# Attention with a gated recurrence on one core: the maxima of the scores are rounded and turned by a rounded product

## The chip, the cores and the metric

One core of a Trainium2 chip runs the whole program in one launch. The metric is device time in microseconds; lower is better. Of several runs the median is given.

## The reference

The input is x of 8 batches with 512 rows of 128. It is normalised by rows (layer norm). Of the result xn two things are computed and added to x: an attention of 16 heads of 64, and a gated recurrence over the 8 batches.

```python
def attn(data, W_qkv, b_qkv, W_out, b_out):      # data: (8, 512, 128)
    qkv = data @ W_qkv + b_qkv                   # 3 * 1024 columns
    q, k, v = (a.reshape(n, l, 16, 64) for a in split(qkv))
    scores = jnp.einsum('nqhd,nkhd->nhqk', q, k)
    attention = jax.nn.softmax(scores / jnp.sqrt(64.), axis=3)
    out = jnp.einsum('nhql,nlhd->nqhd', attention, v).reshape(n, l, 1024)
    return out @ W_out + b_out

def ffn(x, ...):                                 # one step for each batch
    def step(c, xt):
        ft = sigmoid(xt @ wf.T + c @ uf.T + bf)
        it = sigmoid(xt @ wi.T + c @ ui.T + bi)
        gt = tanh(xt @ wc.T + c @ uc.T + bc)
        return ft * c + it * gt, None
    c_final, _ = lax.scan(step, c0, x)
    return tanh(einsum('tbi,oi->tbo', x, wo) + c_final @ uo.T + bo)

result = x + attn(xn, ...) + ffn(xn, ...)
```

## The kernel before

The 16 heads of a batch are 8 pairs; a pair's two heads lie on partitions 0 to 63 and 64 to 127. A batch is 4 stretches (`j` from 0 to 3), each with two pairs, `s` = 2j and 2j + 1; `t` = 8n + s counts the pairs over all batches. The batches run in a loop of the device for n from 1 to 6, with batch 0 and batch 7 written out apart (`batches`). Each engine has its own stream, in an order written out by hand; semaphores join them.

Operands of the scores and projections are split into a rounded part (`QH`, `KH`, `XH`, `WH`, of type float32r) and a rounded rest (`QL`, `KL`, ...), and three rounded products make one. Products of values, of the sums and of the turns take operands of full precision (float32).

For a stretch two pairs ahead, TensorE makes the raw scores of each block of 128 queries once with the rounded parts alone (`score_maxima`, into `mx`), and VectorE takes the largest of each row, negated, into two columns of `NM` (`maxima`, line 592). `NM` is 128x64: two heads, two pairs, four blocks make 16 columns, the others are zero. When a stretch's 16 columns are there, TensorE turns them with one product: `NM` is the stationary operand, the identity the moving one, and 64x128 come out in `mx` (`turn_max`, line 851; for the very first pair `turn_first`, line 926). VectorE copies 16 rows of that into `TM` (`take_max`, line 599, and line 661), two DMAs of SyncE's queue lay them into `MROW`, and the last product of each block's scores adds them to every row (line 871), ahead of the exponential on ScalarE.

At the end of each stretch TensorE runs the values: for each of two pairs, four blocks of keys times two heads (`values`, line 879), the even pair into the bank `pv`, the odd one into `misc`. A product's stationary operand has 64 columns; head 0 goes to partitions 0 to 63 of the bank and head 1 to 64 to 127. The turn for the next stretch stands in the middle of the first pair: `values(n, t, s, (0, 1))`, `turn_max(t + 2)`, `values(n, t, s, (2, 3))`. In the middle of the second pair stand the four sums of the divisors (`four_sums`, line 898) with 32 columns each. There are 33 turns: the first at the start, the second ahead of the first batch's stretch 0, and one in each stretch but the last of batch 7.

What waits near the turn:
- In batches 1 to 7 the values of `misc` wait, in stretch 0, for the tanh of the recurrence, and in stretch 2 for the batch's output rows (`finish`, line 638, VectorE).
- In batch 0 they wait for the state of the recurrence: VectorE runs `take_max`, then `update` (line 573), ScalarE copies and rounds the state (lines 385 and 380), VectorE makes the low half (line 557).
- VectorE's order in stretch 2 is: low halves of two pairs (lines 578, 585), `take_max`, the divisors (line 624), `finish`.

ScalarE begins with seven issues of DMAs, a square root that brings in the table (line 354), and the deviation of batch 0 (`deviation`, line 359). GpSimd makes the identity first (lines 254 to 256), then ones, pads and the zeros of `NM` (line 263).

Of the kernel before, what the change touches and what calls it, by code (L numbers as in the profile page):

```python
# [5 lines left out]
def build_block(nc, data, W_qkv, b_qkv, W_out, b_out, wf, uf, bf, wi, ui, bi, wc, uc, bc, wo, uo, bo, in_c, out):  # L6

    f32 = mybir.dt.float32
    f32r = mybir.dt.float32r
# [4 lines left out]
    P = 128  # L14
# [3 lines left out]
    HD = P // 2  # L18
# [17 lines left out]
    with ctx:  # L36
        def sb(name, shape, dt=f32):
            return ctx.enter_context(nc.sbuf_tensor(name, shape, dt))

        def sem(name):  # L40
            return ctx.enter_context(nc.semaphore(name))

        ident = sb("ident", [P, P])
# [31 lines left out]
        gwL = sb("gwL", [P, 8, P], f32r)  # L75
        DH = sb("DH", [P, L], f32r)
        DL = sb("DL", [P, L], f32r)
        NM = sb("NM", [P, HD])
        TM = sb("TM", [4 * TB, P])
        epst = sb("epst", [P, 1])  # L80
        spare = sb("spare", [P, 2])
# [15 lines left out]
        mx = ctx.enter_context(nc.psum_tensor("mx", [P, 2, L], f32))  # L97
# [21 lines left out]
        ld_b, ld_w, ld_wo = sem("ld_b"), sem("ld_w"), sem("ld_wo")  # L119
        ld_x = [sem("ld_x12"), sem("ld_x34"), sem("ld_x57")]  # L120
        ld_W = [sem("ld_Wq"), sem("ld_Wk"), sem("ld_Wv")]
        id0, id1, ones_set, pads_set, pads_nm, eps_set = sem("id0"), sem("id1"), sem("ones_set"), sem("pads_set"), sem("pads_nm"), sem("eps_set")
        bias_tr, bias_col, bias_half, bias_fold, bias_fin = (sem("bias_tr"), sem("bias_col"), sem("bias_half"),
                                                             sem("bias_fold"), sem("bias_fin"))
        gw_tr, gw_raw, gw_hi, gw_lo = sem("gw_tr"), sem("gw_raw"), sem("gw_hi"), sem("gw_lo")
        first_turned, first_tm, d_first = sem("first_turned"), sem("first_tm"), sem("d_first")
# [16 lines left out]
        q_lo, k_lo, red_done, max_turned, tm_done, den_used, r16_done, rd_done, out_done = (  # L143
            sem("q_lo"), sem("k_lo"), sem("red_done"), sem("max_turned"), sem("tm_done"), sem("den_used"), sem("r16_done"),
            sem("rd_done"), sem("out_done"))
# [107 lines left out]
        def _(pool):  # L253
# [6 lines left out]
            nc.gpsimd.memset(MROW[:, :, :].bitcast(f32), 0.0).then_inc(pads_set, 1)  # L260
            nc.gpsimd.memset(ONEROW[:, :].bitcast(f32), 0.0).then_inc(pads_set, 1)
            pool.wait_ge(pads_set, 2)
            nc.gpsimd.memset(NM[:, :], 0.0).then_inc(pads_nm, 1)
            for h in range(2):
                nc.gpsimd.memset(ONEROW[AUX[h], :].bitcast(f32), 1.0).then_inc(pads_set, 1)
                pool.wait_ge(pads_set, 3 + h)
# [81 lines left out]
        def _(act):  # L348

            act.dma_start(brow[0:3 * PAIRS, :], b_qkv.rearrange("(c r) -> c r", r=P)).then_inc(ld_b, 16)  # L350
            for i, v in enumerate((b_out, bf, bi, bc, bo, in_c)):
                act.dma_start(brow[B_OUT + i:B_OUT + i + 1, :], v.rearrange("(a r) -> a r", a=1)).then_inc(ld_b, 16)
            act.wait_ge(eps_set, 1)
            nc.scalar.activation(spare[:, 0:1], epst[:, :], ACT.Sqrt)

# [165 lines left out]
        def _(dve):  # L521
# [66 lines left out]
            def maxima(t, s, b, turned=0):  # L588

                wait(dve, max_turned, turned)  # L590
                dve.wait_ge(mx_done, 4 * t + b + 1)
                nc.vector.tensor_reduce(NM[:, 0:4 * TB].rearrange("p (h a b) -> p h a b", h=2, a=2)[:, :, s % 2, b],  # L592
                                        mx[:, :, :], AX.X, ALU.max, negate=True).then_inc(red_done, 1)
# [162 lines left out]
        def _(pe):  # L756
# [91 lines left out]
            def turn_max(t):  # L848

                pe.wait_ge(red_done, 4 * t + 8)  # L850
                nc.tensor.matmul(mx[0:HD, 0, 0:P], NM[:, :], ident[:, :], start=True, stop=True).then_inc(max_turned, 1)

            def scores(n, t, s, u, parts=range(4)):

# [68 lines left out]
            def turn_first():  # L923

                pe.wait_ge(red_done, 4)
                nc.tensor.matmul(mx[0:HD, 0, 0:P], NM[:, :], ident[:, :], start=True, stop=True).then_inc(first_turned, 1)

            turn_x(0)
            pe.wait_ge(ld_b, 16 * 7)
# [22 lines left out]
            for c in range(PAIRS):  # L952
                last = nc.tensor.matmul(pv[:, 0:1], WO[:, c, :], bcol[:, B_V + c:B_V + c + 1],
                                        start=(c == 0), stop=(c == PAIRS - 1))
            last.then_inc(bias_fold, 1)
            pe.wait_ge(pads_nm, 1)
            turn_first()
            pe.wait_ge(ones_set, 1)
            pe.wait_ge(pads_set, 4)
# [12 lines left out]
            def step(n, first, last):  # L972
                for j in range(STRETCHES):
# [4 lines left out]
                    if first and j == 0:  # L978
# [23 lines left out]
                        project(0, 3, 0, q_done, first_q[3])  # L1002
                        project(0, 3, DIM, k_done, first_k[3])
                        turn_max(0)
                        pe.wait_ge(q_lo, 3)
                        pe.wait_ge(k_lo, 3)
# [131 lines left out]
                    if coming:  # L1138
                        if first:
                            pe.wait_ge(xl_done, min(s + 3, N))  # L1140
                        turn_max(t + 2)
# [63 lines left out]
```

## Time and profile before

| | |
|---|---|
| median of 3 runs | 889.63 us (889.49 to 891.8) |
| the profiled execution | 892.3 us, its span 890.5 us |
| granted TensorE clock, mean | 0.994 |
| busy: TensorE products | 846.6 us (95%), 5431 records |
| busy: VectorE, ScalarE, GpSimd | 529.0, 450.4, 568.3 us |
| reductions into NM (line 592) | 256, 1226 ns each |
| products of values (line 879) | 1024 records of about 600 ns, 250.9 us busy |

Times of a row count from the span's start. A record of a product is as long as its operands travel through the array; several are under way at once, so what a product costs is the distance from one start to the next, and not its length. A product of full operands has two records, a rounded one has one. The view of the order of time joins neighbours of one kind: "x8" is eight records, and its duration reaches from the first start to the last end. "[0.69 <-PE mx L851]" is idle time of the engine and what ended it.

### The profile page before, as it was taken

To read this page: it belongs to the slowest core of one execution; us is meant where nothing else is said; L and a number is where in the kernel's file an instruction comes from. 1 tells how busy PE (TensorE), PEld (TensorE's weight loads), DVE (VectorE), ACT (ScalarE), POOL (GpSimd) and SP (SyncE) were. 2 spreads that over 40 slices of the span, in tenths; PEclk is the share of its full clock that TensorE was granted. 3 is DMA by queue.
4 is the path that set the end of the run, shared out by engine and by line. 5 is a ranking of instruction groups with operands and counts; after the bars stand their busy time and mean duration, and the time that the engine had idled before them with its cause. 6 is when DMAs were issued, how large, how long until landed. Compare 5 with 4: busy or idle time off the path is not lost.

```text
span 890.5 us, 15128 instructions
## 1 busy us (share of the span) xinstructions
PE 846.6 (95%) x5431; PEld 497.6 (56%) x5431; DVE 529.0 (59%) x687; ACT 450.4 (51%) x585; POOL 568.3 (64%) x299
## 2 busy tenths in 40 slices
PE   6989999999999999999999999999999999999997
PEld 4555566555656545655656645665556645665442
DVE  6676765566466646666466646666466646666422
ACT  5456465455545524555555525555455525555430
POOL 4637684376567647776567647776567647776465
PEclk9899999999999999999999999999999999999999
DMA  8000000000000000000000000000000000000000
GB/s 236 1 1 1 25 1 1 1 14 26 2 14 14 1 25 12 1 13 24 1 13 13 1 24 13 1 13 24 1 13 13 1 24 13 1 14 1 2 25 12
DMA packets 28491, 14.22 MB, mean 16 GB/s; under 512 B 11154, under 2 KB 26032, under 8 KB 28464
## 3 DMA queue, kind: packets, MB, share of 16 engines
q1 hardware_dynamic: 28416, 13.84, 5.4%
q8 instruction: 17, 0.28, 0.1%
q14 instruction: 10, 0.08, 0.0%
q10 hardware_dynamic: 48, 0.02, 0.0%
HBM read 6.83 MB, written 2.10 MB: 10 GB/s over the span
## 4 chain that ended last, share of the span: by engine, by line
PE 86%; DVE 8%; issue 2%; ACT 2%; POOL 2%; DMA 0%; DVEq 0%; POOLq 0%; ACTq 0%
PE st L863 19%; PE misc L879 13%; PE pv L879 9%; PE st L796 9%; PE mx L844 8%; PE st L871 6%; PE mx L905 6%; PE st L898 3%; DVE NM L592 3%; PE pv L796 2%; PE misc L779 2%; PE misc L796 2%; PE pv L779 1%; DVE KL L578 1%; PE mx L779 1%
## 5 line engine op out<-in xcount | busy, mean ns | idle before, releaser
L592 DVE TENSOR_REDUCE NM<-mx 128x2 f32<-128x1024 f32 x256 | 313.9, 1226 | 183.2 <-PE mx L844 183.1
L426 ACT ACTIVATE probs<-st 128x1024 f32<-128x1024 f32 x256 | 256.8, 1027 | 71.5 <-PE st L871 64.9
L309 POOL TENSOR_TENSOR PSUMK<-probs 128x1024 f32<-128x1024 f32 x64 | 153.4, 2397 | 217.8 <-ACT probs L426 217.8
L315 POOL TENSOR_TENSOR PSUMK<-PSUMK,probs 128x1024 f32<-128x1024 f32 x64 | 152.8, 2387 | 6.1
L322 POOL TENSOR_TENSOR PSUMK<-PSUMK,probs 128x1024 f32<-128x1024 f32 x64 | 152.6, 2385 | 6.1
L879 PE MATMUL misc<-probs,VALL 128*64 128x512 f32 x512 | 125.7, 600 | 12.5 <-DVE RES L638 9.5
L879 PE MATMUL pv<-probs,VALL 128*64 128x512 f32 x512 | 125.2, 608 | 0.2 <-DVE RES L563 0.2
L844 PE MATMUL mx<-KH,QH 64*128 64x512 f32 x512 | 108.0, 415 | 6.7 <-DVE NM L592 6.0
L863 PE MATMUL st<-QH,KH 64*128 64x512 f32 x512 | 105.3, 405 | 0.6 <-ACT probs L426 0.6
L863 PE MATMUL st<-QL,KH 64*128 64x512 f32 x512 | 102.0, 393 | 0.0
L863 PE MATMUL st<-QH,KL 64*128 64x512 f32 x512 | 102.0, 392 | 0.0
L871 PE MATMUL st<-MROW,ONEROW 64*128 64x512 f32 x512 | 101.6, 390 | 0.0
L879 PEld LDWEIGHTS misc<-probs,VALL 128*64 128x64 f32 x512 | 44.0, 136 | 85.9 <-issue 51.2
L844 PEld LDWEIGHTS mx<-KH,QH 64*128 64x128 f32 x512 | 48.3, 184 | 62.6 <-issue 28.8
L298 POOL TENSOR_TENSOR AT<-AT,RD 128x512 f32<-128x512 f32 x49 | 61.5, 1274 | 23.8 <-DVE RD L610 12.4
L418 ACT COPY AT<-pv 128x512 f32<-128x512 f32 x25 | 14.7, 588 | 121.8 <-PE pv L879 121.8
L418 ACT COPY AT<-misc 128x512 f32<-128x512 f32 x24 | 14.1, 586 | 108.8 <-PE misc L879 108.8
L863 PEld LDWEIGHTS st<-QH,KH 64*128 64x128 f32 x512 | 48.3, 185 | 36.5 <-ACT probs L426 29.8
L879 PEld LDWEIGHTS pv<-probs,VALL 128*64 128x64 f32 x512 | 44.5, 137 | 42.6 <-issue 31.4
L616 DVE STREAM_TRANSPOSE SD<-st 128x512 f32<-128x512 f32 x28 | 20.1, 717 | 80.8 <-PE st L898 80.8
L905 PE MATMUL mx<-AT,WO 128*128 128x512 f32 x128 | 57.2, 599 | 9.3 <-DVE NM L592 9.3
L871 PEld LDWEIGHTS st<-MROW,ONEROW 64*128 64x128 f32 x512 | 48.7, 184 | 10.6 <-issue 0.4
(183 smaller groups left out, 1221.0 us busy)
## 6 DMA issues: line engine op xcount, KB each, us to landing
XSH<-XH SPq DMA_DIRECT2D x8, 256.0 KB, 2.4
XSL<-XL SPq DMA_DIRECT2D x8, 256.0 KB, 2.4
RES<-in_L_attn_data_dram SPq DMA_DIRECT2D x8, 256.0 KB, 2.8
out_dram<-RES SPq DMA_DIRECT2D x8, 256.0 KB, 2.3
RX<-R SPq DMA_DIRECT2D x112, 2.0 KB, 1.7
probs<-in_L_attn_W_qkv_dram SPq DMA_DIRECT2D x3, 512.0 KB, 5.6
AT<-in_L_attn_data_dram SPq DMA_DIRECT2D x2, 512.0 KB, 7.1
MROW<-TM SPq DMA_DIRECT2D x62, 4.0 KB
```

The costliest lines, as they stand in the source:

```text
L298: nc.gpsimd.tensor_tensor(AT[:, s % PAIRS, :], unnormalised(first, s), RD[:, s % 2, :], ALU.mult).then_inc(norm_done, 1)
L309: nc.gpsimd.tensor_tensor(PSUMK[:, s % 2, :, :], e[:, :, 0, :], e[:, :, 1, :], ALU.add).then_inc(sum_part, 1)
L315: nc.gpsimd.tensor_tensor(PSUMK[:, s % 2, :, :], PSUMK[:, s % 2, :, :], probs[:, s % 2, :, 2, :], ALU.add).then_inc(sum_part, 1)
L322: nc.gpsimd.tensor_tensor(PSUMK[:, s % 2, :, :], PSUMK[:, s % 2, :, :], probs[:, s % 2, :, 3, :], ALU.add).then_inc(sum_done, 1)
L426: nc.scalar.activation(probs[:, s % 2, :, u, :], st[:, u % 2, :, :], ACT.Exp, scale=SCALE).then_inc(exp_done, 1)
L592: nc.vector.tensor_reduce(NM[:, 0:4 * TB].rearrange("p (h a b) -> p h a b", h=2, a=2)[:, :, s % 2, b], mx[:, :, :], AX.X, ALU.max, negate= ...
L796: last = nc.tensor.matmul(dst, stationary[OWN[h], :], moving[OWN[h], :], start=(slot == 0), stop=(slot == 5))
L844: last = nc.tensor.matmul(mx[:, h, :], QH[OWN[h], s % 4, b * P:(b + 1) * P], KH[OWN[h], s % 4, :], start=True, stop=True)
L863: nc.tensor.matmul(st[:, u % 2, h, :], k[OWN[h], s % 4, b], q[OWN[h], s % 4, :], start=(i == 0), stop=False)
L871: last = nc.tensor.matmul(st[:, u % 2, h, :], ONEROW[OWN[h], :], MROW[OWN[h], s % 2, :], start=False, stop=True)
L879: last = nc.tensor.matmul(value_banks[s % 2][OWN[h], :], VALL[:, kb, s * P + h * HD:s * P + (h + 1) * HD], probs[:, s % 2, h, kb, :], star ...
L905: last = nc.tensor.matmul(dst, WO[:, c, :], AT[:, c, :], start=(c == 0), stop=(c == PAIRS - 1))
```

## The change

`NM` becomes float32r, so that VectorE rounds the maxima where it writes them. A second identity, `identr`, of type float32r, is filled once by a copy on ScalarE ahead of the first square root. The turns take `NM` and `identr`; their place in TensorE's stream is the same, and TensorE waits once for `identr` ahead of the first turn.

```diff
-        NM = sb("NM", [P, HD])
+        NM = sb("NM", [P, HD], f32r)
+        identr = sb("identr", [P, P], f32r)
...
-            nc.gpsimd.memset(NM[:, :], 0.0).then_inc(pads_nm, 1)
+            nc.gpsimd.memset(NM[:, :].bitcast(f32), 0.0).then_inc(pads_nm, 1)
...
                 act.dma_start(brow[B_OUT + i:B_OUT + i + 1, :], v.rearrange("(a r) -> a r", a=1)).then_inc(ld_b, 16)
+            act.wait_ge(id1, 1)
+            nc.scalar.copy(identr[:, :], ident[:, :]).then_inc(idr, 1)
             act.wait_ge(eps_set, 1)
...
             def turn_max(t):
 
                 pe.wait_ge(red_done, 4 * t + 8)
-                nc.tensor.matmul(mx[0:HD, 0, 0:P], NM[:, :], ident[:, :], start=True, stop=True).then_inc(max_turned, 1)
+                nc.tensor.matmul(mx[0:HD, 0, 0:P], NM[:, :], identr[:, :], start=True, stop=True).then_inc(max_turned, 1)
...
             def turn_first():
 
                 pe.wait_ge(red_done, 4)
-                nc.tensor.matmul(mx[0:HD, 0, 0:P], NM[:, :], ident[:, :], start=True, stop=True).then_inc(first_turned, 1)
+                nc.tensor.matmul(mx[0:HD, 0, 0:P], NM[:, :], identr[:, :], start=True, stop=True).then_inc(first_turned, 1)
...
             pe.wait_ge(pads_nm, 1)
+            pe.wait_ge(idr, 1)
             turn_first()
```

## Rows read from the trace of the kernel before

**Rows 1.** The page: the chain that ended last, shares by engine.
```profile
PE 86%; DVE 8%; issue 2%; ACT 2%; POOL 2%; DMA 0%; DVEq 0%; POOLq 0%; ACTq 0%
```
**Rows 2.** Line 851: who waited for it (us in total, times).
```profile
  DVE TM L599: 16.2, 12
```
**Rows 3.** Order of time, TensorE, values with a turn: start, us, engine, line.
```profile
322.28 1.94 PE L879 MATMUL pv<-probs,VALL 128*64 128x512 f32 x8
324.04 0.27 PE L851 MATMUL mx<-ident,NM 128*64 128x128 f32 x1
324.05 0.64 PE L879 MATMUL pv<-probs,VALL 128*64 128x512 f32 x1
324.15 0.27 PE L851 MATMUL mx<-ident,NM 128*64 128x128 f32 x1
324.26 1.88 PE L879 MATMUL pv<-probs,VALL 128*64 128x512 f32 x7
325.82 0.75 PE L879 MATMUL misc<-probs,VALL 128*64 128x512 f32 x2
```
**Rows 4.** Order of time, TensorE, last stretch of batch 7: values without a turn.
```profile
873.29 1.02 PE L905 MATMUL mx<-AT,WO 128*128 128x512 f32 x2
874.24 3.65 PE L879 MATMUL pv<-probs,VALL 128*64 128x512 f32 x16
877.73 1.03 PE L889 MATMUL mx<-PSUMK,ones 128*64 128x512 f32 x4
```
**Rows 5.** Order of time, TensorE: rounded and full products follow on one tile.
```profile
868.77 0.39 PE L779 MATMUL misc<-DL,gwH 128*128 128x512 f32 x1
869.00 1.02 PE L905 MATMUL mx<-AT,WO 128*128 128x512 f32 x2
...
42.20 0.60 PE L768 MATMUL mx<-ident,AT 128*128 128x128 f32 x4
42.55 0.48 PE L779 MATMUL mx<-XH,gwH 128*128 128x512 f32 x1
```
**Rows 6.** Order of time, TensorE: the last of the twenty stretches.
```profile
825.38 1.94 PE L879 MATMUL pv<-probs,VALL 128*64 128x512 f32 x8
```
**Rows 7.** Order of time, VectorE and TensorE, stretch 2 of batch 3.
```profile
348.17 0.27 DVE L599 COPY TM<-mx 16x128 f32<-16x128 f32 x1
...
349.58 0.64 DVE L638 TENSOR_TENSOR RES<-misc,RES 128x512 f32<-128x512 f32 x1
...
350.28 0.65 PE L879 MATMUL misc<-probs,VALL 128*64 128x512 f32 x2 [1.54 <-DVE RES L638]
```
**Rows 8.** Order of time, VectorE, batch 0: the copy in stretches 1 and 0.
```profile
99.47 0.28 DVE L599 COPY TM<-mx 16x128 f32<-16x128 f32 x1 [0.69 <-PE mx L851]
...
65.03 0.24 DVE L599 COPY TM<-mx 16x128 f32<-16x128 f32 x1
```
**Rows 9.** TensorE's order of time, busy by window (granted clock 0.51), and the chain.
```profile
22.27 0.58 PE L926 MATMUL mx<-ident,NM 128*64 128x128 f32 x2
...
22.40:25.00 2.60, 1.97 (x10) 0.51 0.01 4
...
37.20 0.36 PE mx L851 x2
```
**Rows 10.** ScalarE: order of time at the start, and one group (count, busy, mean ns).
```profile
3.24 1.28 ACT L354 ACT_TABLE_LOAD   x1 [3.24 <-issue]
...
4.94 0.30 ACT L359 ACTIVATE std<-mv,epst 128x4 f32<-128x4 f32 x1 [0.21 <-DVE mv L530]
5.24 1.04 ACT L368 CAST WH<-probs 128x1024 fp32r<-128x1024 f32 x1
...
L441 ACT COPY bcol<-misc 128x30 f32<-128x30 f32 x1 | 0.2, 192 | 0.0
```
**Rows 11.** VectorE's groups by shape: count, busy, mean ns, idle before.
```profile
L557 DVE TENSOR_TENSOR DL<-misc,DH 128x512 fp32r<-128x512 f32 x8 | 5.5, 686 | 4.6 <-ACT DH L380 4.6
L573 DVE SCALAR_TENSOR_TENSOR misc<-RES,misc 128x512 f32<-128x512 f32 x8 | 5.5, 684 | 0.1
```

More of the change, by code:

```diff
@@ L121, in build_block @@
         ld_W = [sem("ld_Wq"), sem("ld_Wk"), sem("ld_Wv")]
-        id0, id1, ones_set, pads_set, pads_nm, eps_set = sem("id0"), sem("id1"), sem("ones_set"), sem("pads_set"), sem("pads_nm"), sem("eps_set")
+        id0, id1, idr, ones_set, pads_set, pads_nm, eps_set = sem("id0"), sem("id1"), sem("idr"), sem("ones_set"), sem("pads_set"), sem("pads_nm"), sem("eps_set")
         bias_tr, bias_col, bias_half, bias_fold, bias_fin = (sem("bias_tr"), sem("bias_col"), sem("bias_half"),
```

## The prediction

> **What bounds the kernel now.** I read the page first: its chain that ended last lies on TensorE for 86% of the span [rows 1], so a saving counts only where TensorE is neither waiting nor about to wait. Next who waited for line 851, the turn of the maxima: the copy into TM on VectorE, 12 times, 16.2 us together [rows 2]. Then the order of time around one turn, in batch 3 [rows 3]. Here the reader must see two streams. A product of values is 64 columns wide, and head 0 goes to the lower, head 1 to the upper half of the array; they start in pairs. The turn fills the lower half alone, and is two records, as every product of full operands is. It starts at 324.04, its second record at 324.15, and the lower half's next product of values at 324.26: the turn costs the lower half 0.22 us. The upper half starts its own product at 324.05 in the turn's shade; that record is 0.64 us long where the others are 0.59, so it bears a late weight load of 0.05. The values of the other bank start at 325.82, 3.54 after the first; the pair's row ends 0.75 later, and a record is 0.59, so the lower half starts 0.16 behind, at 325.98, 3.70 after the first. The last batch has a stretch of values without a turn: its 16 records take 3.49 (874.24 to 877.73) [rows 4]. So the turn makes the upper half 0.05 and the lower half 0.21 longer. The four sums behind these values use another width of tile, and wait for both halves; the lower one decides.
>
> **What a product of rounded operands costs.** A full 512-column record has a pitch of 0.43 (two of them end after 1.02, and one is 0.59 long), and a rounded one on the same tile 0.23, from 868.77 to 869.00 [rows 3, 5]. A full product is two such records, so about four passes against one. A turn has 128 columns: its two records have a pitch of 0.109 each (0.22 for both, rows 3), which is two passes of about 0.055. One pass leaves the lower half with 0.055 in place of 0.218: a gain of 0.163 per turn where the lower half decides. The load of the next weights, 64 columns wide, must fit under that one pass: the exposed load was 0.05 (0.64 against 0.59) [rows 3], so it just fits. If it does not, up to 0.05 of the gain is gone. The other half keeps its 0.05 at worst and is then level with the lower one, so it does not take the bound over.
>
> **Where the gain counts.** There are 33 turns, and each has its place.
> - Batches 1 to 7, stretches 0, 1 and 3, except stretch 3 of batch 7, which has no turn: 20 turns. In all of them the second bank follows without a wait, 3.54 after the first bank's start; rows 3 are one, and the last starts at 825.38 [rows 6]. 20 x 0.163 = 3.26 us.
> - Batches 1 to 7, stretch 2: 7 turns. Here the second bank waits for the sum of the output rows on VectorE, RES, and TensorE starts at 350.28 after 1.54 idle, so the values of the first bank were long through. The copy into TM stands ahead of that sum at 348.17, but without a wait: it follows VectorE's own work, not the turn [rows 7]. What is late next here is the same VectorE chain, so the gain is 0.
> - Batch 0, stretches 1 to 3: the copy into TM does wait, 0.69 at 99.47, and behind it on VectorE are queued the update of the recurrence and the low half of the state, for which TensorE's second bank waits. The stream ends 0.163 earlier, so the copy does. 3 x 0.16 = 0.49. In stretch 0 the copy at 65.03 follows other VectorE work with no wait [rows 8]: 0.
> - The turn ahead of the first step stands alone on the chain, 0.36 for two records at 37.20; 0.16 off it. The very first one, at 22.27, takes 0.58 for two records, at a clock that is granted at 0.51 in the 2.6 us from 22.4, the lower of the two levels (1.2 GHz); with one record I take 0.2, between the 0.16 of the full clock and the 0.32 of the half [rows 9].
>
> **What is added.** First, a rounded copy of the identity, 128x128, on ScalarE, ahead of the first table load. A copy of 30 columns took 0.19 and one of 1024 columns 1.04, so 0.85 ns for each column more; 128 columns give 0.27. It pushes the load of 1.28 at 3.24 back, and the deviation behind it, at 4.94, which is on the way to the first product. But that one waited 0.21 for VectorE [rows 10]. So 0.27 less 0.21 is 0.06 of delay; bounds 0 and, were the table to be loaded twice, 1.28 + 0.06 = 1.34. The copy waits for the identity, which GpSimd has ready before ScalarE has issued its seven DMAs, so nothing is queued behind an open wait; none of the queues of DMAs is passed. Second, TensorE waits for that copy only ahead of the first turn, at 22.27, when it has long been made: nothing. Third, the maxima are written in the rounded type: VectorE's results of that type take 686 ns where those of the full type take 684, same size [rows 11], so the 256 reductions stay as they are; a change of 1 ns in each would be 0.3 us in all at most. The memset writes the same bytes.
>
> **The sum.** 3.26 + 0.49 + 0.16 + 0.20 - 0.06 = 4.05 us. The profiled execution has a span of 890.5 and took 892.3; it would take 888.3. The median of the runs shown is 889.63, 2.7 lower, and the same difference makes 885.6.
>
> The Trainium skill ("TensorE: Matmul & The Clock Gate", Back-to-back issue gap) gives a stream of load and product pairs at 128 columns some 81 ns each, where a lone product would be some 56. By that the turn would cost the lower half 0.081, and, called an estimate, the twenty turns give 20 x 0.137 = 2.7. The row at 324.04 to 324.15 shows only the two-pass record.
>
> **The rivals.**
> First, on the other side: the array drains when the precision changes. A drain can be priced: from records 128 columns wide to values 64 wide the pitch is 0.52 (873.29 to 874.24 is 0.95 for two, one of them 0.43) [rows 4], so 0.09 more, and the record behind it bears the exposed 0.05. Two such switches around the turn, 0.28, and the turn's 0.055 hold up both halves by 0.34, where now the lower one loses 0.21: 0.13 more on 20 turns, +2.5; in batch 0 the two effects cancel. That gives 892.1. It becomes a loss once a switch costs more than 0.08. Against it: the rounded product at 868.77 is followed by a full one at 869.00 on the same tile with the ordinary 0.23, and the transposes, full type, by a rounded product at 42.55, when the fourth of them had only just started (0.60 for all, 0.27 for one, so at 42.53) [rows 5]. But both are the whole array, not two halves of which only one changes its type.
> A rule of the Trainium skill ("TensorEngine Tiling (Array Packing)", Key Properties) is that changing the tiling mode drains TensorE. By that rule, the 0.52 at 874.24 is such a drain; whether a type counts as a mode the page does not say.
>
> Second, the change doesn't do what it says: 128 columns of rounded operands run no faster than full ones. Every rounded product in the trace has 512 columns, so no row excludes it. Then the turn costs what it did: 889.6, give or take 0.4.
>
> Third, the pitch is not the pass but a floor: the four transposes of 128 columns take one record each and still stand 0.11 apart (42.20 to 42.53) [rows 5]. Then only one record goes, 0.109 on 20 turns, 2.2, and about 0.5 in batch 0: 886.9. They load 128 columns of weights each, though, and the turn 64, so I hold this to be less likely.
>
> Fourth, the table is loaded a second time: 885.6 + 1.3 = 886.9.
>
> **How the numbers follow.** The forecast, 885.6 with its own range of 884.6 to 887.0, gets 0.55; drains, 892.1, 0.12; no change, 889.6, 0.12; the floor, 886.9, 0.14; the second table load, 886.9, 0.07. The range of 884.4 to 890.0 leaves out the drains and the tails of the forecast. 0.3% is about what a measurement of this kernel can tell from no change, and that is 2.7 us: the line lies at 886.96. Most of the forecast is below it (0.52 of 0.55), and half of the floor and of the table load (0.10 together): faster 0.63, within 0.3% 0.25, slower 0.12.
>
> **What the profile afterwards would show.** In a stretch of values: one record of the turn, the lower half's next product 0.055 behind it (a pitch of 0.11 speaks for the floor, 0.22 for the second rival), the second bank's pair together at about 3.54, and the four sums 0.16 earlier after the first value. A turn whose neighbours on the upper half are both late, or a first record of 0.64 in both halves, shows a drain. In stretch 2 the second bank must still start behind RES, at the same distance from the last maxima. On ScalarE there is one table load ahead of the first deviation, and the deviation begins at about 5.0. The forecast is wrong if the twenty stretches are not shorter by 0.16, or if they are and a wait behind them, for the sums of GpSimd or the low halves of VectorE, takes the time back.

## The result

Over 16 runs each the changed kernel takes 894.43 us (median, 892.7 to 897.52) and the kernel before 891.17 us (889.49 to 893.05); the ratio is 1.004, with an interval of 1.0028 to 1.0052. It is slower by about 3.5 us. The profiled execution has a span of 892.3 us.

The order of time on TensorE around the turn of batch 3, in the changed kernel (start, us, engine, line; "x8" are eight records):

```profile
321.80 1.94 PE L882 MATMUL pv<-probs,VALL 128*64 128x512 f32 x8
323.67 0.27 PE L854 MATMUL mx<-identr,NM 128*64 128x128 f32 x1
323.87 1.94 PE L882 MATMUL pv<-probs,VALL 128*64 128x512 f32 x8
325.64 1.89 PE L882 MATMUL misc<-probs,VALL 128*64 128x512 f32 x8
327.45 1.06 PE L901 MATMUL st<-PSUMK,ones 128*32 128x512 f32 x8
```

and the row of the four sums in the kernel before, which [rows 3] stop short of:

```profile
327.79 1.07 PE L898 MATMUL st<-PSUMK,ones 128*32 128x512 f32 x8
```

The turn is one record, as meant. But against [rows 3] three things are new. The turn starts 1.87 after the first value, where it was 1.76: the array runs empty ahead of it. No value starts in its shade; the next ones, of both halves, stand 0.20 behind it. And all eight records behind it take 1.94, as the first eight of the bank do (321.80); three steps of 0.43 and a record of 0.59 would make 1.88, so the first pair bears the exposed weight load of 0.05. The second bank starts 3.84 after the first in place of 3.54. Its two halves are level now, which gives 0.16 back, so from the first value to the four sums it is 5.65 in place of 5.51 (327.45 - 321.80 and 327.79 - 322.28): 0.14 lost in each of the twenty stretches. The total can be read off the first value of the first of them and the four sums of the last, in the changed kernel:

```profile
190.04 0.65 PE L882 MATMUL pv<-probs,VALL 128*64 128x512 f32 x2
...
832.56 1.07 PE L901 MATMUL st<-PSUMK,ones 128*32 128x512 f32 x8
```

and in the kernel before:

```profile
191.18 1.94 PE L879 MATMUL pv<-probs,VALL 128*64 128x512 f32 x8
...
830.89 1.06 PE L898 MATMUL st<-PSUMK,ones 128*32 128x512 f32 x8
```

The changed kernel is 1.14 ahead at the first and 1.67 behind at the last: 2.81 us lost in between, 20 x 0.14.

Stretch 2 is as it was, with the second bank behind RES, and VectorE's rows keep their distances ([rows 7]); in batch 3 the turn is off the path there:

```profile
349.28 0.64 DVE L641 TENSOR_TENSOR RES<-misc,RES 128x512 f32<-128x512 f32 x1
...
349.97 0.65 PE L882 MATMUL misc<-probs,VALL 128*64 128x512 f32 x2 [1.40 <-DVE RES L641]
```

And ScalarE's start, which answers to [rows 10]:

```profile
3.21 1.28 ACT L355 ACT_TABLE_LOAD   x1 [3.21 <-issue]
4.51 0.30 ACT L355 CAST identr<-ident 128x128 fp32r<-128x128 f32 x1
4.82 1.28 ACT L357 ACT_TABLE_LOAD   x1
...
6.23 0.28 ACT L362 ACTIVATE std<-mv,epst 128x4 f32<-128x4 f32 x1
```

The copy brings a table of its own, the square root behind it another, and the deviation begins at 6.23 in place of 4.94. VectorE's reductions take 1226 ns, as before.

That the changed kernel is nevertheless 1.14 ahead at 190 us is for the most part the clock of this one execution. The granted clock between 23.9 and 27.3 is 0.50, the lower level (1.2 GHz), and it rises there; in the kernel before it was at 0.51 from 22.4 to 29.3, twice as long. By an estimate from these rows, 3.5 us less at half the clock are worth up to 1.7, the first two turns give up to 0.6 back (below), and the second table load takes 1.2 to 1.3 (6.23 against 4.94): 1.1 in all. How long the clock stays down differs between executions. In the traces of this document the stretch at the start is 6.8 to 6.9 us long, 3.4, or absent, and most have a second one of 3.4 us near the end (from 848.4 in the kernel before, from 849.9 in the changed one). The mean granted clock of a run counts both. So runs are compared below at equal mean granted clock too.

### The profile page after: what moved, and what is told of

Read it like the earlier page. It is cut to its first block, busy times and chain, and to the rows that moved or that the text cites. A ratio compares the mean times of both kernels' runs of the same rounds, so it can differ in the third digit from the quotient of the medians.

```text
span 892.3 us, 15064 instructions
## 1 busy us (share of the span) xinstructions
PE 847.9 (95%) x5398; PEld 471.4 (53%) x5398; DVE 529.1 (59%) x687; ACT 451.7 (51%) x587; POOL 568.3 (64%) x299
## 4 chain that ended last, share of the span: by engine, by line
PE 86%; DVE 7%; ACT 2%; issue 2%; POOL 2%; ACTq 0%; DVEq 0%; POOLq 0%
PE st L866 19%; PE misc L882 13%; PE pv L882 9%; PE st L799 9%; PE mx L847 8%; PE st L874 6%; PE mx L908 6%; PE st L901 3%; DVE NM L595 3%; PE misc L799 2%; PE misc L782 2%; PE pv L799 2%; PE pv L782 1%; DVE KL L581 1%; PE mx L782 1%
## 5 line engine op out<-in xcount | busy, mean ns | idle before, releaser
L595 DVE TENSOR_REDUCE NM<-mx 128x2 fp32r<-128x1024 f32 x256 | 313.9, 1226 | 181.5 <-PE mx L847 181.3
L882 PE MATMUL misc<-probs,VALL 128*64 128x512 f32 x512 | 122.6, 600 | 11.1 <-DVE RES L641 8.7
L882 PEld LDWEIGHTS misc<-probs,VALL 128*64 128x64 f32 x512 | 33.5, 136 | 94.9 <-issue 74.1
L882 PEld LDWEIGHTS pv<-probs,VALL 128*64 128x64 f32 x512 | 31.3, 137 | 52.9 <-issue 49.0
```

Source lines behind the costliest of these rows:

```text
L882: last = nc.tensor.matmul(value_banks[s % 2][OWN[h], :], VALL[:, kb, s * P + h * HD:s * P + (h + 1) * HD], probs[:, s % 2, h, kb, :], star ...
```

## The experiments

Two theories. A, precision: any change of type in a stream of 64-column products drains the array. B, mode: a rounded product of 64 columns doesn't keep to its half but runs over the whole array, so it needs another mode than the values on either side, and it is the mode that drains.

### The pitches by themselves

The kernel before, with this behind its last product on TensorE (`F` is a pair of full products of 64 weight columns, `F128` and `R128` full and rounded ones of 128, `small` one product of 128 moving columns, `rid` and `bid` the rounded and the bfloat16 identity; the latter lies in a tile named TG):

```diff
+            F(16)
+            small(ident, HD)
+            F(2)
+            small(rid, HD)
+            F(2)
+            small(bid, HD)
+            F(2)
+            small(ident, HD, is_transpose=True)
+            F(2)
+            small(rid, HD)
+            small(rid, HD)
+            small(rid, HD)
+            small(rid, HD)
+            F(2)
+            small(rid, P)
+            F(2)
...
+            F128(2)
+            small(rid, HD)
+            F128(2)
+            small(ident, HD)
+            F128(2)
+            small(bid, HD)
+            F128(2)
...
+            R128(4)
+            small(rid, HD)
+            R128(2)
+            small(ident, HD)
+            R128(2)
+            small(bid, HD)
+            R128(2)
```

> The kernel before, with a row of products behind its last one on TensorE: pairs of full products of 64 columns (the shape of the values), between them one small product of 128 moving columns at a time (full, rounded, bfloat16, a transpose of full type; 64 or 128 weight columns), then the same small ones among full products 128 weight columns wide, then among rounded ones 128 wide. Their results are not used. Theory A, precision: every change of type in a stream of 64-column products drains the array, so the rounded and the bfloat16 small product both stand 0.52 behind the product of values ahead of them and hold up both halves, by about 0.34 against a stream without them; four rounded ones in a row are 0.055 apart. Theory B, mode: the rounded product of 64 columns runs over the whole array, so it drains among the values (0.52), but not among products 128 weight columns wide, full or rounded (0.43 and 0.23, as without it), where a full product of 64 columns does drain (0.09 more); a bfloat16 product of 64 columns keeps its half and does not drain among the values. Under A the rounded 64-column product among full ones 128 wide would drain too.

The order of time, first among pairs of 64 columns, then among full and among rounded products of 128:

```profile
900.56 0.27 PE L1204 MATMUL mx<-ident 128*64 128x128 f32 x1
...
900.78 1.88 PE L1192 MATMUL pv<-AT,VALL 128*64 128x512 f32 x7
902.59 0.27 PE L1204 MATMUL mx<-rid 128*64 128x128 f32 x1
902.79 1.94 PE L1192 MATMUL pv<-AT,VALL 128*64 128x512 f32 x8
904.56 0.22 PE L1204 MATMUL mx<-TG 128*64 128x128 bf16 x1
904.57 1.93 PE L1192 MATMUL pv<-AT,VALL 128*64 128x512 f32 x8
906.43 0.30 PE L1204 MATMUL mx<-ident 128*64 128x128 f32 x1
906.66 1.94 PE L1192 MATMUL pv<-AT,VALL 128*64 128x512 f32 x8
908.53 0.45 PE L1204 MATMUL mx<-rid 128*64 128x128 f32 x4
...
919.29 1.45 PE L1196 MATMUL pv<-AT,WO 128*128 128x512 f32 x3
920.18 0.62 PE L1204 MATMUL mx<-rid 128*64 128x128 f32 x1
920.64 1.93 PE L1196 MATMUL pv<-AT,WO 128*128 128x512 f32 x4
922.50 0.43 PE L1204 MATMUL mx<-ident 128*64 128x128 f32 x2
922.86 1.99 PE L1196 MATMUL pv<-AT,WO 128*128 128x512 f32 x4
924.77 0.24 PE L1204 MATMUL mx<-TG 128*64 128x128 bf16 x1
924.95 1.98 PE L1196 MATMUL pv<-AT,WO 128*128 128x512 f32 x4
...
926.37 1.49 PE L1200 MATMUL pv<-XH,WH 128*128 128x512 f32 x4
927.70 0.22 PE L1204 MATMUL mx<-rid 128*64 128x128 f32 x1
927.76 0.68 PE L1200 MATMUL pv<-XH,WH 128*128 128x512 f32 x2
928.37 0.43 PE L1204 MATMUL mx<-ident 128*64 128x128 f32 x2
```

The full product (900.56 to 900.78) repeats [rows 3]. The rounded one (902.59) has the next pair 0.20 behind it, as in the changed kernel. The bfloat16 one (904.56) has a value of the upper half beside it at once (904.57), and no drain. The transpose (906.43) has its next pair 0.23 behind it.

The length of a merged row gives the drain ahead. Eight values, all started, end 0.59 after the last start. Behind the bfloat16 turn they run from 904.57 to 906.50, so the last start is at 905.91, and the transpose stands 0.52 behind it; the pitch without a drain is 0.43. In the same way the rounded product at 902.59 is 0.52 behind the last value: 900.78 + 1.88 - 0.59 = 902.07.

Four rounded turns in a row end after 0.45, so with 0.22 for the last one they start in 0.23: 0.11 and then 0.06 apart. So a product of 128 rounded columns is one pass of about 0.06, as forecast.

A rounded product that has 128 weight columns, and so needs the whole array beyond doubt, does to the values what the one of 64 columns does: it starts at 910.78, 0.52 behind the last value (908.91 + 1.94 - 0.59 = 910.26), and the next pair stands at 911.04, 0.26 behind it.

The last two blocks decide between A and B. Among full products of 128 columns, the rounded one of 64 columns starts in their shade (920.18, its predecessor at 919.29 + 1.45 - 0.59 = 920.15) and the next comes at 920.64, 0.49 behind that: 0.06 more than 0.43, the pass alone, though the type changes twice. (Its own start, 0.03 behind its predecessor's, is no measure of its cost: right behind a full product on the whole array a rounded record starts early, 0.03 behind again at 926.37 and, in the last experiment, at 318.61, and what follows bears the pitch.) The full product of 64 columns drains, without any change of type: 922.50 is 0.52 behind 921.98 (920.64 + 1.93 - 0.59), and the next product stands 0.36 behind its start. Among rounded ones the same: 0.06 for the rounded one (927.70 to 927.76), 0.36 for the full one (928.37, and the next at 928.73). The bfloat16 one of 64 columns drains here too: 924.77 is 0.51 behind 924.26 (922.86 + 1.99 - 0.59), and the next product stands 0.18 behind it. Theory A falls. 64-column products of full type and in bfloat16 need the mode of half the array, since each drains among whole-array products and not among the values; the rounded one does the reverse, so it runs in the mode of the whole.

The tiling page of the Trainium skill ("TensorEngine Tiling (Array Packing)", Key Properties) says that changing the mode, not just the tile, drains TensorE. By that rule, the trace agrees, 0.52 in place of 0.43 each time; that a rounded product of 64 columns counts as the mode of the whole array is what the pitches add.

### The changed kernel with the product in full precision

```diff
-  nc.tensor.matmul(mx[0:HD, 0, 0:P], NM[:, :], identr[:, :], ...)
+  nc.tensor.matmul(mx[0:HD, 0, 0:P], NM[:, :].bitcast(f32), identr[:, :].bitcast(f32), ...)
```

> The changed kernel, with the rounded maxima and the rounded identity, but the product that turns them takes them as full operands again (two records). If the switches around the rounded product are the loss, the 20 stretches are back at 8.37 from the first bank's start to the next maxima, and what is left of the change is the second table load: 0.2 to 0.5 us slower than before (ratio 1.000 to 1.001). If something in the writing of the rounded maxima costs, it stays at 1.003 to 1.004.

891.81 us, ratio 1.0017 (1.0008 to 1.0025): about 1.5 us slower than before, and not the 3.5 of the changed kernel. The stretch is back at [rows 3]: the second bank starts 3.54 after the first.

```profile
323.53 1.94 PE L882 MATMUL pv<-probs,VALL 128*64 128x512 f32 x8
...
327.07 1.02 PE L882 MATMUL misc<-probs,VALL 128*64 128x512 f32 x3
```

This stretch is 1.25 later than in the kernel before (322.28), in two executions whose clock was down equally long at the start (6.8 and 6.9 us), and the copy still brings a table load of its own (two loads of 1.28, at 3.21 and 4.82). I had expected at most 0.5 of it to come through; it comes through nearly whole. So writing rounded maxima costs nothing that shows, and the second table load costs about 1.3 us.

### The turn in bfloat16

```diff
-        NM = sb("NM", [P, HD])
+        NM = sb("NM", [P, HD], bf16)
+        identb = sb("identb", [P, P], bf16)
...
+            pool.wait_ge(id1, 1)
+            nc.gpsimd.tensor_copy(identb[:, :], ident[:, :]).then_inc(idr, 1)
...
-  nc.tensor.matmul(mx[0:HD, 0, 0:P], NM[:, :], ident[:, :], ...)
+  nc.tensor.matmul(mx[0:HD, 0, 0:P], NM[:, :], identb[:, :], ...)
```

> The kernel before, with the maxima and the identity in bfloat16; the copy of the identity is on GpSimd, so there is no second table load. The scores are shifted by a coarser maximum, which softmax cancels. Theory B: no drain, the lower half gives 0.055 to the turn in place of 0.218, 20 x 0.16 = 3.2 and about 0.7 in batch 0: 3.9 us faster (ratio 0.9956). Theory A: drains as in the changed kernel, 3.0 slower (ratio 1.003).

885.85 us, against 890.49 for the kernel before on the same chip: ratio 0.9952 (0.9939 to 0.9965), 4.3 us faster. Some of that is the clock, since its five runs lie at 0.996 to 0.998 and most of the others at 0.995: at equal clock it is 3.6 faster (0.997, one run each) and 4.1 (0.998, three each), against the 3.9 expected.

```profile
318.04 1.94 PE L883 MATMUL pv<-probs,VALL 128*64 128x512 f32 x8
319.81 0.22 PE L855 MATMUL mx<-identb,NM 128*64 128x128 bf16 x1
319.82 1.93 PE L883 MATMUL pv<-probs,VALL 128*64 128x512 f32 x8
321.53 1.93 PE L883 MATMUL misc<-probs,VALL 128*64 128x512 f32 x8
323.39 1.06 PE L902 MATMUL st<-PSUMK,ones 128*32 128x512 f32 x8
```

Here is the profile that the prediction had described for the rounded turn: the upper half goes on beside it, the second bank starts 3.49 after the first, and the four sums come 5.35 after the first value, where the kernel before has 5.51 and the changed one 5.65. The maxima only shift the exponents, and softmax cancels a shift, so a coarser maximum serves. This version beats both kernels.

### The turn as a transpose

```diff
-  nc.tensor.matmul(mx[0:HD, 0, 0:P], NM[:, :], ident[:, :], ...)
+  pe.sem_inc(passed_pe, 1)
+  nc.tensor.transpose(mx[0:HD, 0, 0:P], NM[:, :], ident[:, :])
```

> The kernel before, the turn as a transpose of full type: one record, no change of type, nothing rounded. Where TensorE's stream waits for a count that is held in a register, an increment of a semaphore carries the wait. If a transpose keeps the half (theory B leaves that open, theory A says so), the turn costs 0.055 to 0.11 in place of 0.218: 2 to 4 us faster (ratio 0.9955 to 0.9975). If a transpose runs over the whole array, it drains like the rounded product: 2.5 to 3 us slower (ratio 1.003).

The very first turn is changed likewise; the increment of a semaphore carries the wait. 893.55 us, ratio 1.0038 (1.0025 to 1.0051). The transpose has one record and the type of the values, and it drains all the same: the next pair of values stands 0.23 behind it.

```profile
322.14 0.30 PE L852 MATMUL mx<-ident,NM 128*64 128x128 f32 x1
322.37 1.94 PE L880 MATMUL pv<-probs,VALL 128*64 128x512 f32 x8
```

It stands 0.51 behind the last value ahead of it (320.28 + 1.94 - 0.59 = 321.63), and the four sums, at 325.96, come 5.68 after the first value: 0.17 more than before. The increment ahead of it isn't the cause, since the transpose of the pitches has none and shows the same 0.52 and 0.23. So it doesn't take rounding to leave the half mode; a transpose of full type does it too.

### Where the rounded identity is made

First by GpSimd, then by ScalarE but behind its first square root:

```diff
-            act.wait_ge(id1, 1)
-            nc.scalar.copy(identr[:, :], ident[:, :]).then_inc(idr, 1)
...
+            pool.wait_ge(id1, 1)
+            nc.gpsimd.tensor_copy(identr[:, :], ident[:, :]).then_inc(idr, 1)
```

> The changed kernel, but GpSimd makes the rounded identity. One table load is left ahead of the first deviation, which begins at about 4.94 as before. Left of the change are the drains, 20 x 0.15 = 3.0 slower, and the first two turns in one pass, up to 0.7 faster: 2.3 to 3.0 slower than before (ratio 1.0026 to 1.0034), and 1.2 to 1.5 faster than the changed kernel.

```diff
-            act.wait_ge(id1, 1)
-            nc.scalar.copy(identr[:, :], ident[:, :]).then_inc(idr, 1)
             act.wait_ge(eps_set, 1)
             nc.scalar.activation(spare[:, 0:1], epst[:, :], ACT.Sqrt)
+            act.wait_ge(id1, 1)
+            nc.scalar.copy(identr[:, :], ident[:, :]).then_inc(idr, 1)
```

> The changed kernel, the rounding copy still on ScalarE, but behind the first square root in its stream. If the second table load comes because a copy stands ahead of the first function that needs a table, there is one load now, and the deviation begins at 5.0 to 5.1 (0.3 for the copy less 0.2 of wait): ratio 1.0026 to 1.0036, level with the kernel whose copy is on GpSimd. If a copy always brings its own table, there are two or more loads and the ratio stays at 1.004.

893.87 us, ratio 1.0035 (1.0021 to 1.005), and 892.57 us, ratio 1.0033 (1.0018 to 1.0048). Where GpSimd makes the identity there is one load, and the deviation begins at 4.83. With the copy behind the square root there is one load too, and the deviation begins at 4.81, earlier than the 5.0 to 5.1 expected:

```profile
3.22 1.28 ACT L355 ACT_TABLE_LOAD   x1 [3.22 <-issue]
...
4.62 0.28 ACT L357 CAST identr<-ident 128x128 fp32r<-128x128 f32 x1
4.81 0.29 ACT L362 ACTIVATE std<-mv,epst 128x4 f32<-128x4 f32 x1
```

These ratios alone don't tell the two from the changed kernel, since their intervals overlap with its, and 1.0035 lies just above the 1.0026 to 1.0034 expected. The runs scatter with the mean granted clock; grouped by it, they read (mean us of the runs, their number):

| kernel | clock 0.995 | clock 0.997 |
|---|---|---|
| before | 890.70 (14) | 889.42 (2) |
| changed | 894.31 (3) | 893.16 (4) |
| changed, full product | 891.83 (7) | 890.70 (1) |
| turn in bfloat16 | | 885.84 (1) |
| changed, GpSimd makes the identity | | 891.63 (3) |
| changed, copy behind the square root | | 892.05 (4) |
| transpose | 893.84 (3) | 893.08 (1) |
| turns of stretches 0 and 1 moved (below) | 888.76 (3) | |

The runs of the kernel before are those measured beside the last three variants; those beside the first four give 890.71 (11) and 889.40 (1). At 0.997 the changed kernel is 3.7 slower than before, and 2.2 or 2.6 without the second table load, so that load is worth 1.1 to 1.5; at 0.992 and 0.993, where 6 runs of the changed kernel lie (897.02 and 895.98 on average), the two variants with one load (896.06 and 894.84 with GpSimd's copy, 896.25 at 0.992 with the copy behind the square root) are only 0.8 to 1.1 faster. The groups are small; the differences agree with the traces, and by themselves would not carry it. I take about 1.3, the 1.25 of the traces among them, with 0.8 to 1.5 as what the runs allow.

### The turn moved to where the mode changes anyway

```diff
                         recurrence(3, n - 1, h_done, N)
+                        turn_max(t + 2)
...
                         project_out(mx[:, 1, :])
+                        turn_max(t + 2)
...
                     values(n, t, s, (0, 1))
...
-                        turn_max(t + 2)
+                        if first or j >= 2:
+                            turn_max(t + 2)
                     values(n, t, s, (2, 3))
```

> The kernel with the rounded turn and GpSimd's copy; in batches 1 to 7 the turns of stretches 0 and 1 stand ahead of the values instead of in their middle, behind a product that runs over the whole array (the recurrence, the output projection). Theory B, mode: no drain ahead of the turn there (0.23 or 0.43 behind the product before it), and the one between it and the values is there anyway, so 13 of the 20 turns cost about 0.06 in place of 0.21: 13 x 0.15 = 2.0 faster than before and 7 drains of 0.15 = 1.0 slower; with the first turns' 0.6, some 1.5 faster (ratio 0.998), unless the wait for the last maxima in stretch 0, up to 0.3 each, takes up to 2 of it back. Theory A, precision: a drain between turn and values and one ahead of it: no better than the changed kernel (ratio 1.003).

The edit is made in the variant with GpSimd's copy. 889.55 us, against 890.54 for the kernel before: ratio 0.9983 (0.9971 to 0.9996), and 1.9 faster at a clock of 0.995. It moves 14 of the twenty turns (two in each of batches 1 to 7), not the 13 of the expectation. A rounded turn that stands behind a product over the whole array costs next to nothing:

```profile
318.58 0.59 PE L908 MATMUL mx<-AT,WO 128*128 128x512 f32 x1
318.61 0.62 PE L854 MATMUL mx<-identr,NM 128*64 128x128 f32 x1
319.16 3.65 PE L882 MATMUL pv<-probs,VALL 128*64 128x512 f32 x16
322.64 1.89 PE L882 MATMUL misc<-probs,VALL 128*64 128x512 f32 x8
```

and in stretch 0 of batch 1, behind the rounded products of the recurrence:

```profile
188.33 0.22 PE L854 MATMUL mx<-identr,NM 128*64 128x128 f32 x1
188.48 3.65 PE L882 MATMUL pv<-probs,VALL 128*64 128x512 f32 x16
```

In stretch 1, from the last output product to the values it is 0.58, where it was 0.52 without a turn between them ([rows 4], 873.29 to 874.24 with 0.43 for the other record); the values then run their 3.48 with nothing in them, and the four sums come 5.30 behind the first (at 324.46). The switch that was there already serves the turn. The wait for the last maxima in stretch 0, which I had feared, didn't show: the turn starts 0.23 behind the last product of the recurrence (188.10), the ordinary pitch, and the values 0.15 behind the turn; without a turn between them these stood 0.31 apart (190.87 and 191.18 in the kernel before). The same product, in the same two types, is 0.14 dearer than the full one in one place and 0.15 cheaper in the other (5.65 and 5.30 + 0.06, against 5.51); what differs is its neighbours' mode.

## Why the prediction was wrong

The forecast was 885.6 us and faster; it is slower, and beyond the range's end of 890.0. Two of the four rivals came true at once, which no case had allowed for: the drain (given 0.12) and the second table load (0.07). Of the 8.8 between the two numbers 1.5 is the start of the sum: it set out from 889.63, the median of 3 runs, and over 16 runs the kernel before takes 891.17. The rest is a gain of 4.05 that came as a loss. Point by point:

- **What bounds the kernel.** The two streams, the turn's 0.22 on the lower half alone, and the twenty stretches in which it counts were right. The loss of 2.81 arises in just these, and the bfloat16 turn makes just these shorter, 5.35 for 5.51.
- **The price of the product** was right for the product: one pass of 0.06. The step that failed is the sentence after it, "one pass leaves the lower half with 0.055 in place of 0.218". It took for granted that the rounded product stays in its half because the full one does. The trace writes both as 128*64, the shape of the operands; it doesn't write the mode.
- **The evidence against the drain was read too wide.** The changes of type without a drain in [rows 5] are all over the whole array. (The rounded product at 42.55 starts 0.02 behind the last transpose, which proves little, as its start is early like the one at 920.18 above; but the next, at 42.87, stands 0.34 behind that transpose, its 0.11 and the 0.23 of a rounded product, so there is no drain.) The text said itself that none was between halves, and still gave the drain 0.12. The kernel before has no rounded product of 64 columns, so no row of it could have told the mode. The changed kernel shows it at the second turn, which follows a rounded product over the whole array. It stands 0.23 behind that, the ordinary pitch, where the full one stood 0.33 behind it, and the 0.09 of a drain comes at what follows, 0.15 behind the turn. The changed kernel, and behind it the kernel before:

```profile
36.01 0.39 PE L763 MATMUL st<-XL,WH 128*128 128x512 f32 x1
36.24 0.22 PE L854 MATMUL mx<-identr,NM 128*64 128x128 f32 x1
36.39 0.50 PE L799 MATMUL pv<-WH,XSH 64*128 64x512 f32 x1
...
36.80 0.40 PE L760 MATMUL st<-XL,WH 128*128 128x512 f32 x1
37.13 0.43 PE L851 MATMUL mx<-ident,NM 128*64 128x128 f32 x2
37.49 0.50 PE L796 MATMUL pv<-WH,XSH 64*128 64x512 f32 x1
```

- **The rival's price** was close: +2.5 for the drains, against 2.81 measured. A turn lost 0.14, where the rival had 0.13, and its parts, 0.09 for a switch and 0.05 for the exposed load, are the ones seen.
- **Batch 0.** "The stream ends 0.163 earlier, so the copy does" failed for the same reason: the drain ahead of the turn takes what the one pass gives, and the lead of the changed kernel's copy over the one before hardly moves: 1.08 in stretch 0 (65.03 and 63.95) and 1.10 in stretch 3 (168.28 and 167.18). In the bfloat16 kernel the lead grew over the same three stretches from 3.13 (61.90) to 3.61 (164.67), so by 0.48, the 0.49 of the forecast.
- **The table.** The copy's own time was right (0.30 for 0.27), and the rival had priced a second load at 1.34, near the 1.3 or so measured; that it would come was held unlikely. The rows at the start show every copy of ScalarE behind the square root's load, so they couldn't tell that one ahead of it asks for a table.
- **The first two turns** gave more than the 0.16 and 0.20 of the sum. At the second, from the product ahead of it to the one behind it, it was 0.69 (36.80 to 37.49) and is 0.38 (36.01 to 36.39): 0.31 off, since the drain ahead of it goes too. At the first, from the turn to the next product, it was 1.21 (22.27 to 23.48) and is 0.90 (22.78 to 23.68), but part of this 0.31 is the clock, which was down in the one and not yet in the other.
- **The sum as it came:** 2.8 for the drains, 1.3 for the table, and up to 0.6 back from the first two turns, so about 3.5 at equal clock, against the 3.6 between 890.70 and 894.31 at 0.995.

What stays open: why the transpose and the rounded product leave the half mode and bfloat16 doesn't; the runs show that they do. The trace doesn't write the mode, so it is read off the pitches alone.

## What to carry to other kernels

A cheaper product isn't cheaper where it stands among products of another mode: read which products run side by side on parts of the array, and put a lone one of another kind next to a change of mode that is there anyway, or give it a type that keeps the mode. A value that only shifts an exponent can be bfloat16, as long as its rounding is small against the range of the exponential; no run here tries larger scores. A new operation on ScalarE belongs behind the first function that loads a table, not ahead of it.

## What the runs showed of the hardware

- A rounded (float32r) product with 64 weight columns runs in the mode of the whole array: behind full products of 64 columns it starts 0.52 after the last of them in place of 0.43, and the next ones of the half mode 0.20 after it, with an exposed weight load of 0.05. Among products of 128 columns it costs 0.06 and no drain, and there the full one of 64 columns costs 0.45 (0.09 ahead of it and 0.36).
- A full transpose of 64 weight columns drains among full products of 64 columns in the same way (0.52 and 0.23); a bfloat16 product of 64 columns doesn't drain there, but does among products of 128 columns (0.51 and 0.18).
- The granted clock was at 0.50 to 0.51 for 6.9 or 3.4 us near 25 us, or not at all, and in most executions for 3.4 us near 850.
- A copy that is the first operation of ScalarE's stream brings a table load of 1.28 us, and the square root behind it another; behind the square root's load it brings none.
